# Conditioned feed-forward stage on one core: time and scale operands from token columns with a table lookup on TensorE, instead of gathered rows that are transposed

## The reference, cut to what matters

```python
h = _ln(x, pw_g[pathway_ids], pw_b[pathway_ids])
h = _ln(h, cp_g[compartment_ids], cp_b[compartment_ids])
t = _ln(x, tm_g[time_steps], tm_b[time_steps])
s = _ln(x, ms_g[scale_type], ms_b[scale_type])
...
cat = jnp.concatenate([w[0]*h, w[1]*t, w[2]*m, w[3]*n, w[4]*r, w[5]*s], axis=-1)
return _mlp_ln(cat, int_W1, int_b1, int_W2, int_b2, int_g, int_be)
```

## Time and profile before

| | us |
|---|---|
| median of 3 runs (1750.16 to 1752.95) | 1752.3 |
| the profiled execution | 1750.74 |
| its span in the profile | 1748.8 |
| last stage (from the first main to the end) | about 535 |
| TensorE busy, of the span | 1733.7 |

### The profile page before, as it was taken

One profiled execution on the slowest core, in us unless ns is written; L12 is line 12 of the kernel. 1 busy time (PEld: TensorE's weight loads), 2 busy tenths in 40 slices (PEclk: granted clock), 3 DMA queues, 4 the chain that ended last, 5 costly groups with the idle time before them and its releaser, 6 DMA issues. The chain is left out here.

```text
span 1748.8 us, 23364 instructions
## 1 busy us (share of the span) xinstructions
PE 1733.7 (99%) x7935; PEld 1407.0 (80%) x7935; DVE 1192.6 (68%) x1756; ACT 878.1 (50%) x1301; POOL 786.8 (45%) x702
## 2 busy tenths in 40 slices
PE   9999999999999999999999999999999999999998
PEld 7888888888778888888888888778877787787786
DVE  8756667669989678786563335357886687587555
ACT  7655555565666565674562223243453443443433
POOL 1112221122766566665560000025577877878742
PEclk9999999999999999999999999999999999999999
DMA  6011110120233324222536568877645445544511
GB/s 208 1 49 49 48 39 9 49 73 25 97 132 119 134 97 168 97 97 85 187 139 222 193 197 281 325 254 245 217 132 183 143 159 175 155 159 152 170 38 61
DMA packets 121991, 234.36 MB, mean 134 GB/s; under 512 B 25618, under 2 KB 25874, under 8 KB 121892
## 3 DMA queue, kind: packets, MB, share of 16 engines
q1 hardware_dynamic: 91732, 157.63, 27.0%
q0 software_dynamic: 11776, 41.95, 7.0%
q10 hardware_dynamic: 18384, 33.56, 5.8%
HBM read 170.71 MB, written 58.72 MB: 131 GB/s over the span
## 5 line engine op out<-in xcount | busy, mean ns | idle before, releaser
L1070 PE MATMUL bank<-h_parts,mlp_w 128*128 128x512 f32 x2016 | 460.0, 389 | 4.6 <-DVE mlp_w L1493 3.3
L1070 PEld LDWEIGHTS bank<-h_parts,mlp_w 128*128 128x128 f32 x2016 | 378.0, 188 | 85.4 <-DVE mlp_w L1493 3.7
L353 PE MATMUL bank<-h_parts,gate_w 128*128 128x512 f32 x1536 | 351.1, 389 | 0.6 <-DVE h_parts L688 0.5
L353 PEld LDWEIGHTS bank<-h_parts,gate_w 128*128 128x128 f32 x1536 | 288.1, 188 | 61.9 <-issue 0.9
L2066 PE MATMUL bank<-operand_parts,int_w 128*128 128x512 f32 x1152 | 279.8, 396 | 0.5 <-DVE u_tiles L2716 0.4
L1135 PE MATMUL bank<-p_parts,mlp_out_w 128*128 128x512 f32 x1152 | 271.2, 393 | 0.0
L1135 PEld LDWEIGHTS bank<-p_parts,mlp_out_w 128*128 128x128 f32 x1152 | 213.8, 188 | 48.4 <-issue 4.2
L2066 PEld LDWEIGHTS bank<-operand_parts,int_w 128*128 128x128 f32 x1152 | 212.2, 188 | 47.1 <-issue 2.2
L615 POOL TENSOR_TENSOR decay_sq<-decay 128x512 f32<-128x512 f32 x32 | 39.3, 1227 | 278.8 <-DVE decay L701 278.8
L1408 POOL TENSOR_TENSOR product_out<-product_out,gelu 128x512 f32<-128x512 f32 x69 | 120.0, 1762 | 97.1 <-DVE product_out L1564 96.6
L1288 ACT ACTIVATE product_copy<-bank,vec_sb 128x512 f32<-128x512 f32 x144 | 99.1, 688 | 112.4 <-PE bank L1070 111.4
(11 more groups left out here) (311 smaller groups left out, 2760.4 us busy)
## 6 DMA issues: line engine op xcount, KB each, us to landing
p_tile<-p_d ACTq DMA_DIRECT2D x96, 256.0 KB, 4.8
p_d<-product_out SPq DMA_DIRECT2D x92, 256.0 KB, 2.0
raw_mlp_w<-mlp_gate_g SPq DMA_DIRECT2D x21, 512.0 KB, 3.7
raw_mlp_w<-mlp_fc_g SPq DMA_DIRECT2D x21, 512.0 KB, 4.4
xin<-xT SPq DMA_DIRECT2D x8, 1024.0 KB
hs_d<-u SPq DMA_DIRECT2D x8, 1024.0 KB, 5.0
hs_pair<-hs_d SPq DMA_DIRECT2D x8, 1024.0 KB, 7.5
x_columns<-xT SPq DMA_DIRECT2D x8, 1024.0 KB, 6.9
```

The lines of the kernel that those rows point to most:

```text
L353: i = pe.matmul(bank[:], gw[:, w, s, k, m * P:(m + 1) * P], hr[:, q, t, k, :], start=k == 0 and n == 0, stop=k == KT - 1 and n == 2)
L1070: i = pe.matmul(bank[:], wb[g % 2][:, s, w, kk, :], hop[u % 2][o][:, t, kk, :], start=first and kk == 0 and n == 0, stop=kk == 1 and n == ...
```

## The change

Time and scale operands are made in channel columns from the start. The mean and reciprocal root of each token of x, so far [128 tokens x 4], are stored to DRAM (`store_stats`) and loaded again as rows of 512 tokens spread over all 128 partitions (`load_stats`). GpSimd makes xhat in columns from the x_columns tiles (`xhat_columns`: one multiply, one add for each of 4 slices), slices 0 and 1 at the end of the block before and 2 and 3 at its start. The gain of each channel and token comes from one matmul with 32 contracted rows, gain table by one-hot, into a ring bank (`emit`). VectorE multiplies bank by xhat column (`gain_product`) into SBUF, and front_high and front_low then read SBUF. The gather of rows, the products on rows, and the transposes of tt and ts are gone. Items of t and s stand in two groups of four, before main 6 and before main 10, and the bias matmuls move from behind main 8 to right behind the second group. In block 0 the table is split into high and low part once.

```diff
+        def store_stats(b):
+            sp.wait_ge(S["x_rs"], 2 * (b + 1))
+            for c, t in enumerate((rstd, shift)):
+                sp.dma_start(stats_d[c].rearrange("(n p) -> p n", p=P)[:, TT * b:TT * (b + 1)], t[:, XS, :],
+                             allow_slow_non_contiguous=True).then_inc(stats_stored, 16)
+
+        def load_stats(b):
+            sp.wait_ge(stats_stored, 32 * (b + 1))
+            if b:
+                sp.wait_ge(xn_add, KT * b)
+            for c in range(2):
+                sp.dma_start(spread[:, c, :], stats_d[c:c + 1, bass.ts(b, BT)].partition_broadcast(P)).then_inc(stats_loaded, 16)
...
             residual(0)
             residual(1)
+            if nxt:
+                store_stats(b + 1)
             turn(0)
+            if nxt:
+                load_stats(b + 1)
             if nxt2:
                 sp.wait_ge(S["xh_done"], TT * (b + 2))
                 load(b + 2)
...
+            elif kind in ("tt", "ts"):
+                if isinstance(b, int) and b == 0:
+                    pe.wait_ge(gain_done, 1)
+                pe.wait_ge(S["oh_done"], b + 1)
+                group, c = gain_of(kind, k)
+                i = pe.matmul(dst[:], gains[group, c, :], oh[group, :], start=True, stop=True, tile_position=(group.start, 0))
...
+    ITEMS_AT = {2: (4, 5), 4: (6, 7), 6: (8, 9, 10, 11), 10: (12, 13, 14, 15)}
+    GAINS_AT = {6: (8, 9), 7: (10, 11), 10: (12, 13), 11: (14, 15)}
+    BIAS_AT = 10
...
         def load_x(b, k):
             if k < 2:
                 act.wait_ge(S["op_low"], NS * (b - 1) + k + 3)
+                act.wait_ge(xn_mul, KT * (b - 1) + k + 3)
             else:
                 act.wait_ge(S["op_low"], NS * b + k - 1)
+                act.wait_ge(xn_mul, KT * b + k - 1)
...
-        def gather_ts(b, t, first):
...
-        def scale_rows(b):
...
+        def xhat_columns(b, k):
...
+            pool.wait_ge(stats_loaded, 32 * (b + 1))
+            pool.tensor_tensor(xn[:, k], x_columns(b, k), spread[:, 0, :], ALU.mult).then_inc(xn_mul, 1)
+            pool.wait_ge(xn_mul, KT * b + k + 1)
+            pool.tensor_tensor(xn[:, k], xn[:, k], spread[:, 1, :], ALU.add).then_inc(xn_add, 1)
...
-        def t_product(b, t):
...
+        def gain_product(b, s):
+            o, k = steps[s]
+            dve.wait_ge(S[FRONT[o] + "_ps"], KT * b + k + 1)
+            dve.wait_ge(xn_add, KT * b + k + 1)
+            dve.tensor_tensor(source(b, s), xn[:, k], bank(FRONT[o], k)[:], ALU.mult).then_inc(S[o + "_prod"], 1)
...
         def front_low(b, s):
-            o, k = steps[s]
             dve.wait_ge(S["op_high"], NS * b + s + 1)
-            dve.tensor_tensor(op[:, s % 4, 1, :], x_columns(b, k) if o == "x" else bank(FRONT[o], k)[:],
-                              op[:, s % 4, 0, :].bitcast(F32), ALU.subtract).then_inc(S["op_low"], 1)
+            dve.tensor_tensor(op[:, s % 4, 1, :], source(b, s), op[:, s % 4, 0, :].bitcast(F32), ALU.subtract).then_inc(S["op_low"], 1)
```

More of the change, by code:

```diff
@@ L1805, in conditioned_ffn @@
     OH_AT, ROW_AT = 4, 6
-    T_AT = 0
     QT_AT, FF_AT = 8, 10
@@ L1815, in add_items @@
         o, k = steps[s]
-        items.append((FRONT[o], k, ("op_low", NS, s, 0)))
+        items.append((FRONT[o], k, {"h": ("op_low", NS, s, 0), "t": ("t_prod", KT, k, 0), "s": ("s_prod", KT, k, 0)}[o]))
     order = []
     for s in range(NS):
[L1820 to L1823, removed]
+        for later in ITEMS_AT.get(s, ()):
+            add_items(later)
+            order.append(("item", len(items) - 1))
         order.append(("main", s))
@@ L1844, in conditioned_ffn, with gain_of, source @@
     FREED = {2: 1, 3: 2, 6: 3, 7: 4}
+    def gain_of(kind, k):
+        group = (2 * k + (kind == "ts")) % 4
+        return slice(GROUP * group, GROUP * (group + 1)), k // 2
+    def source(b, s):
+        o, k = steps[s]
+        if o == "x":
+            return x_columns(b, k)
+        return {"h": lambda: bank("th", k)[:], "t": lambda: tn[:, k % 2], "s": lambda: xn[:, k]}[o]()
     def item_no(kind, k):
@@ L1898, in body @@
             if isinstance(b, int) and b == 0:
+                store_stats(1)
+                load_stats(1)
                 sp.wait_ge(S["xh_done"], TT * 2)
@@ L2052, in main @@
             o, k = steps[s]
+            if s == BIAS_AT:
+                if isinstance(b, int) and b == 0:
+                    pe.wait_ge(tab_done, 1)
+                pe.wait_ge(S["oh_done"], b + 1)
+                for m in range(KT):
+                    rows_m = slice(GROUP * m, GROUP * (m + 1))
+                    pe.matmul(A[m][:], bias_t[rows_m, :], oh[rows_m, :], start=False, stop=False, tile_position=(GROUP * m, 0))
             if isinstance(b, int) and b == 0:
@@ L2067, in main @@
                                   start=s == 0 and n == 0, stop=False)
-            if s == NS // 2:
-                if isinstance(b, int) and b == 0:
-                    pe.wait_ge(tab_done, 1)
-                pe.wait_ge(S["oh_done"], b + 1)
-                for m in range(KT):
-                    rows_m = slice(GROUP * m, GROUP * (m + 1))
-                    i = pe.matmul(A[m][:], bias_t[rows_m, :], oh[rows_m, :], start=False, stop=False,
-                                  tile_position=(GROUP * m, 0))
             i.then_inc(S["z_ps"], 1)
@@ L2663, in moments @@
             dve.wait_ge(S[pre + "_ag"], TT * (b + 1))
+            if which == XS and not (isinstance(b, int) and b == 0):
+                dve.wait_ge(stats_stored, 32 * b)
             dve.tensor_scalar(rstd[:, which, :], mv[:, which, :, 1], 1e-5, None, ALU.add).then_inc(S[pre + "_ve"], 1)
@@ L2752, in steps_of @@
                     table_rows_now(b + 1)
-                if T_AT <= s < T_AT + TT:
-                    t_product(b, s - T_AT)
+                for later in GAINS_AT.get(s, ()):
+                    gain_product(b, later)
                 if nxt and X_AT <= s < X_AT + TT:
@@ L3076, in lay_out @@
     arrays["cp_rows"] = np.repeat(c2["cp_g"], NMS, axis=0)
-    arrays["ts_rows"] = np.concatenate([np.repeat(c2["tm_g"], NMS, axis=0), np.tile(c2["ms_g"], (NCP, 1))], axis=1)
+    gain_rows = np.zeros((4, 32, 2, P), np.float32)
+    for k in range(KT):
+        part = slice(k * P, (k + 1) * P)
+        gain_rows[2 * k % 4, :2 * NCP, k // 2] = np.concatenate([c2["tm_g"][:, part]] * 2)
+        gain_rows[(2 * k + 1) % 4, 2 * NCP:NOH, k // 2] = np.concatenate([c2["ms_g"][:, part]] * 2)
+    arrays["gain_rows"] = gain_rows.reshape(P, 2 * P)
     b16 = np.stack([five(c2["cp_b"])[:NOH], five(c2["tm_b"])[:NOH], three(c2["ms_b"])[:NOH]])
```

116 lines of the change are left out of this document (63 added, 53 removed).

## The result

The changed kernel takes 1867.92 us (median of 4 runs, 1859.18 to 1868.83) against 1752.62 (1750.16 to 1754.06): ratio 1.0649, 95% interval 1.063 to 1.0667. It is **slower by 115 us**; the forecast was 8 us faster, and the range ended at 1757.

The account below looks back on a forecast made before the run. TensorE was taken as the bound, with GpSimd's hidden chain a second one just under it. Middle blocks -12.7 and block 0 +4.0 sum to -8.7 us, giving 1744 us, range 1736 to 1757.

Parts of the forecast that it names:

- two stores issue in 1.4 and land about 3.4 after the root for x: DMA issues of store_stats: two stores of 512 4-byte pieces, timed from a load of short pieces (0.68 issue, 2.7 landing).
- 3 us if small stores go slower than small loads: Upper bound on the delay of x_tiles and the second transpose behind load_stats; lower bound 0, some 1.5 us expected.
- idle of over 1 us before the ff items: Sign of a wrong forecast: TensorE idle there, released by transposed tiles, would mean the DMA queue decides.
- The count is even: GpSimd: eight column operations at 1.30 replace four products and four gathers, 10.4 against 10.4, so it starts blocks earlier.
- the lock at the eight low parts of t and s: VectorE: these now read two SBUF tiles, 0.684 to 1.397 each; bounds 0 and 5.7 us a block, 2 taken, in idle time.
- Some 1.5 us: Delay of x_tiles and the second transpose by load_stats' 0.5 MB, on DMA engines shared with GpSimd's pw_rows.
- Setting it off against GpSimd's earlier start: Blocks 3 to 5: load_stats' extra traffic taken to cancel GpSimd's earlier start; bounds 1.0 us less, 1.5 us more.
- TensorE's gain: Fewer transposes against two lookup groups costing 1.9 to 2.3: 1.9 to 2.35 us a block saved, taken as 2.1.
- -12.7: Sum for blocks 1 to 7: -2.7, -2.0, -1.1, -1.1, -1.6, and -2.1 each for blocks 6 and 7.
- Block 0: Loses 4.0 us, bounds +2 and +7: TensorE waits before the second peak item for VectorE's product on time_columns.
- the hidden chain grows: Rival, chance 0.20: port locks and pw_rows landing late delay the root for h; at 3 us later, +8, 1760.
- -2.1 in all: Blocks 6 and 7 together, in the 1760 sum of the rival "the hidden chain grows".

Follow-up runs that it names:

- e2: The changed kernel without the two stores, its row factors loaded from a row of x1T_d instead (other numbers): 1783.5 us.
- e18: The kernel before plus the stores alone, read by nobody, 1024 pieces of 4 bytes a block, each 512 bytes from the next in DRAM: 1753.4 us.
- e9: e2 with GpSimd's eight column operations cut to one column of 512 from block 1 on: 1769.6 us.
- e5: The changed kernel with 16-byte store pieces, GpSimd waiting for the block's fourth hidden low part before the next block's first two normalised columns: 1807.2 us.
- e15: e9 with VectorE's low parts of t and s cut to one column and factors loaded to 8 partitions, from block 1 on: 1747.4 us, ratio 0.9971.
- e10: The kernel before plus the stores alone, read by nobody, as 256 pieces of 16 bytes a block: 1753.1 us.
- e17: The kernel before plus stores of each block's first tile's factors only, read by nobody, 256 pieces of 4 bytes side by side: 1821.3 us.

## Why the prediction was wrong

**The step that failed** is "two stores issue in 1.4 and land about 3.4 after the root for x", together with its "3 us if small stores go slower than small loads" as the worst delay behind it. It took the duration from a load of short pieces and carried it over to a store of neighbouring 4-byte pieces, a kind of which the trace had no row. The load that waits for them was issued 20.2 us behind them, and pw_rows and the transposes were held up meanwhile: 84 of the 115 us. With the 29 of e2 that is nearly all. No row stood behind the 3 us: the nearest one differed in direction and in address pattern. By e18 it is the addresses that matter. The list of signs ("idle of over 1 us before the ff items") did name where it would show.

**GpSimd.** "The count is even" (10.4 against 10.4) counted occupancy. What went was four products, and gathers and waits, beside which the hidden low part took 0.69; what came was eight operations on SBUF, four of them placed at the hidden low parts. Some 13 us (e2 to e9).

**VectorE.** The prediction put the lock at the eight low parts of t and s, in idle time, and looked for harm at the h chain. In e2, blocks 1 to 6, those of time_columns take 0.71 and those of xhat_columns 1.52 on average, over the 1.397 of its bound, but with 3.5 us a block in all inside the 5.7. (In the changed kernel, where the stores drain, they are 0.68 and 1.37.) But in e2 the hidden low parts, untouched by the change, doubled and lay on the path. The rule of the Trainium skill ("SBUF — State Buffer", "SBUF: two separate sides"), that a VectorE operation with two SBUF inputs and a GpSimd operation lock each other out, agrees with the trace: a hidden low part takes 1.6 us beside GpSimd's columns, 0.69 without them (e5). It belongs to every pair that the new work can meet, not only to the edited lines.

**Loads.** "Some 1.5 us" for the 0.5 MB of factors was right in size: GpSimd waited 3.18 us for pw_rows in a middle block of e9, 1.66 before. Setting it off against GpSimd's earlier start was wrong: together with the low parts of t and s it holds 22 us (e9 to e15).

**Right.** TensorE's gain: block 7, which has no next block, reaches its second matmul after 50.74 us instead of 53.42, 2.68 for the forecast 2.1, and above its 2.35 (from 1479.52 to 1497.39 in the changed kernel's block 3, 72 matmuls and both groups take 17.87 us, 1.4 more than such 72 alone by the earlier trace rows, where 1.9 to 2.3 were put down). The middle blocks of e15 are 62.79, 64.35, 62.56, 62.93, 62.67 and 62.13, which against before, with block 7's 2.7, sums to -12.8 where -12.7 was forecast. That match is in part luck and no proof of the sum: e15 has left out much of the work that the sum counted as free. Block 0 there is 4.9 us longer (forecast 4.0), by a standstill of 3.4 us, though for the reading of the first peak item (rhs_peak) and not at the second. The rival "the hidden chain grows" was the right family, port locks and a later root for h, but it did not name the hidden low parts and was priced at 1760; in e2 the root comes 2.4 us later and the time is 1783. (Its sum takes blocks 6 and 7 at "-2.1 in all", the forecast at -2.1 each; that is a matter of 2 us.)

## What to carry to other kernels

Price a transfer from a row of its own kind: same direction, same piece size, same neighbourhood of addresses; where there is none, the upper bound is open. One longer piece for each partition (e10) or pieces far apart (e18) made the store free here, though the reader of the new layout can pay. When work moves onto an engine whose SBUF work slows another's (here 0.69 to 1.6 us), look at what runs beside the new place, not only at the lines edited. In a kernel that is full on one engine, two small delays can hide each other, so take them away together before calling either free.

## What had not been expected of the hardware

256 pieces of 4 bytes a block side by side in DRAM cost 68 us over the kernel, 1024 of them 512 bytes apart nothing, 256 of 16 bytes side by side nothing; while the slow ones drain, GpSimd waits for row gathers of another queue up to 12.5 us (e17), up to 16.7 in the changed kernel. And a standstill of 10.5 us was followed by twelve matmuls in 4.78 instead of 3.02 us.
